# Expert attention: transposed second forming of the scores against row probabilities that TensorE transposes

## The reference, cut to what matters

```python
def _encoder_layer(x, iw, ib, ow, ob, l1w, l1b, l2w, l2b, n1w, n1b, n2w, n2b):
    b, s, d = x.shape                 # s = 112, d = 256
    hd = d // H                       # H = 16 heads of 16
    qkv = x @ iw.T + ib
    q, k, v = jnp.split(qkv, 3, axis=-1)
    rs = lambda t: t.reshape(b, s, H, hd).transpose(0, 2, 1, 3)
    q, k, v = (rs(q), rs(k), rs(v))
    scores = jnp.einsum('bhqd,bhkd->bhqk', q, k) / jnp.asarray(hd, x.dtype) ** 0.5
    attn = jax.nn.softmax(scores, axis=-1)
    o = jnp.einsum('bhqk,bhkd->bhqd', attn, v).transpose(0, 2, 1, 3).reshape(b, s, d)
    o = o @ ow.T + ob
    x = _layernorm(x + o, n1w, n1b)
    ff = jax.nn.relu(x @ l1w.T + l1b) @ l2w.T + l2b    # inner width 1024
    return _layernorm(x + ff, n2w, n2b)
```

## Time and profile before

| | |
|---|---|
| median of 3 runs | 3894.98 us |
| profiled execution | 3896.07 us |
| its span | 3894.4 us |
| TensorE busy | 3612.2 us, 93% |
| VectorE busy | 1980.3 us, 51% |
| ScalarE busy | 1434.1 us, 37% |
| POOL busy | 371.6 us, 10% |
| mean granted TensorE clock | 0.967 |
| expert stage, first to last TensorE work | 2734.7 to 3883.4 us |

### The profile page before, as it was taken

The page is one execution under the profiler, slowest core; times in us unless marked ns, Lnnn a source line. Parts: engine busy times, 40 slices in busy tenths (PEclk is TensorE's granted clock), DMA queues, the critical chain, the costliest instruction groups (busy, mean ns, idle before and its releaser), DMA issues. The chain is left out here.

```text
span 3894.4 us, 81102 instructions
## 1 busy us (share of the span) xinstructions
PE 3612.2 (93%) x32871; PEld 2736.2 (70%) x32871; DVE 1980.3 (51%) x5378; ACT 1434.1 (37%) x3167; POOL 371.6 (10%) x455
## 2 busy tenths in 40 slices
PE   6999999999699898989898989994899999999997
PEld 4777777777576666666666666662788887878886
DVE  3665656566235353535353534452455555556554
ACT  2343344334134233333333343432344443444443
POOL 1111111111000000000000000000011111111111
PEclk9999999999699999999999999997899999999999
DMA  2000000000200001010101010001300001110000
GB/s 76 12 12 13 14 12 12 14 14 8 88 11 13 24 11 25 9 27 9 28 5 31 1 35 1 25 1 54 129 16 12 11 17 50 54 52 12 15 12 8
DMA packets 63555, 94.55 MB, mean 24 GB/s; under 512 B 7762, under 2 KB 59602, under 8 KB 62146
## 3 DMA queue, kind: packets, MB, share of 16 engines
q1 hardware_dynamic: 55074, 83.41, 6.9%
q0 software_dynamic: 8224, 7.36, 1.7%
HBM read 72.07 MB, written 18.37 MB: 23 GB/s over the span
## 5 line engine op out<-in xcount | busy, mean ns | idle before, releaser
L1478 PE MATMUL bps<-BXT,Bwexp 128*128 128x112 f32 x3072 | 379.7, 282 | 6.2 <-DMA Bwexp<-in_we 3.6
L1478 PEld LDWEIGHTS bps<-BXT,Bwexp 128*128 128x128 f32 x3072 | 361.7, 195 | 22.1 <-issue 9.3
L1243 DVE CUSTOM_DVE_ANT_0 PON<-pps,PMR 112x375 f32<-112x375 f32 x512 | 259.7, 544 | 194.3 <-PE pps L967 192.9
L1096 ACT ACTIVATE PPT<-pps,mcol 125x896 f32<-125x896 f32 x192 | 192.4, 1007 | 204.6 <-PE pps L986 204.4
L1564 PE MATMUL bps<-Bwexp,BPT 128*112 128x256 f32 x1024 | 235.9, 380 | 0.0
L657 POOL TENSOR_TENSOR rstd<-var,nhalf 112x1 f32<-112x1 f32 (+1 forms) x96 | 148.3, 1545 | 838.6 <-DVE var L575 459.1
L967 PE MATMUL pps<-PKT,PQM 64*112 64x375 f32 x1024 | 211.1, 501 | 6.0 <-DVE Pmx L1243 4.0
L1276 POOL TENSOR_TENSOR Prstd<-Pvar,nhalf 112x1 f32<-112x1 f32 x128 | 70.1, 548 | 1517.9 <-DVE Pvar L1164 1517.9
L1618 ACT ACTIVATE BPT<-bps,Bwexp 128x112 f32<-128x112 f32 x512 | 139.1, 354 | 170.9 <-PE bps L1478 170.9
L1564 PEld LDWEIGHTS bps<-Bwexp,BPT 128*112 128x112 f32 x1024 | 174.5, 177 | 35.3
L986 PE MATMUL pps<-PQM,PKT 64*125 64x448 f32 x768 | 187.5, 567 | 0.0
(11 more groups left out here) (302 smaller groups left out, 7280.8 us busy)
## 6 DMA issues: line engine op xcount, KB each, us to landing
Bwexp<-in_we SPq DMA_DIRECT2D x7, 2304.0 KB, 17.0
PCX<-in_ctx SPq DMA_DIRECT2D x32, 375.0 KB
BXIN<-xmid SPq DMA_DIRECT2D x64, 112.0 KB
out<-BY POOLq DMA_DIRECT2D x64, 112.0 KB, 2.9
Bwexp<-in_we SPq DMA_DIRECT2D x7, 777.0 KB, 4.6
wa_sb<-in_wa SPq DMA_DIRECT2D x1, 4736.0 KB, 14.8
Brexp<-in_re SPq DMA_DIRECT2D x7, 672.0 KB
XIN<-in_x SPq DMA_DIRECT2D x32, 112.0 KB
```

Of the source, the lines that this page charges most:

```text
L1096: A(PT[s][0:KP, k, :, :].rearrange("p (i v) q -> p i (v q)", i=2), PS[s][0:KP, :, 0:QW], ACT.Exp, bias=mcol[:, k, bass.ds(at.n[s] + s * qu ...
L1243: m = v.tensor_tensor_reduce(out=ON[s][0:T, i * LC:(i + 1) * LC], in0=bank[s][i][0:T, 0:LC], in1=MR[s][:, :], scale=1.0, scalar=-3.0e38, o ...
L1478: m = mm(o[:, j * T:(j + 1) * T], wt[:, c, n0 + j * 128:n0 + (j + 1) * 128], rhs[:, c, :], start=(c == 0), stop=(c == 1))
```

## The change

Scores are formed once, with the queries in the partitions. Of each half of eight heads VectorE takes the maxima and multiplies them by -0.25 (low). ScalarE then runs one exp a head (112x112) with low as its bias column and accum_out for the row sums, so eight for a half. VectorE takes the reciprocal of the sums and multiplies the half by it in place. TensorE transposes eight heads at a time back into the lane's banks, ScalarE copies each half to PT. The values lie in V48, 48 columns for two heads: 16 of the one, 16 zeros, 16 of the other. A window of 32 of these columns is the weights of one head, and two heads add into the same 32 partitions. The product thus comes out with its features in the partitions, and OT is read from it directly. Gone are the transposed maxima, the selector matmuls, the second forming of the scores, the ones column, the transposes back to rows, ON and its transposes.

The diff, without the semaphore names and with the tables of three engines:

```diff
@@ -84,27 +84,27 @@
-    "lead3": (0, 264, 500, 764),
...
+    "lead3": (0, 262, 500, 762),
...
+    "pe3": ((30, 71, 245, 266, 466, 515, 687, 756, 775, 837, 875, 904, 987, 988,),
+            (30, 42, 106, 285, 371, 523, 610, 737, 757, 826, 883, 883, 960, 976,),
+            (30, 89, 255, 270, 436, 496, 555, 578, 800, 969, 979, 979, 996, 996,),
+            (30, 74, 171, 287, 479, 595, 644, 790, 819, 854, 889, 889, 898, 898,)),
+    "act3": ((0, 79, 204, 259, 491, 491, 705, 743, 791, 861, 888,),
+             (8, 25, 132, 320, 395, 510, 560, 602, 797, 913, 945,),
+             (1, 40, 225, 348, 391, 497, 568, 586, 817, 919, 955,),
+             (1, 32, 103, 338, 519, 593, 730, 761, 839, 846, 877,)),
+    "dve3": ((10, 85, 220, 250, 456, 702, 720, 720, 915, 974,),
+             (52, 210, 259, 259, 321, 593, 607, 665, 851, 923,),
+             (68, 278, 315, 375, 432, 612, 626, 834, 834, 870,),
+             (10, 150, 313, 351, 493, 730, 732, 779, 782, 860,)),
...
@@ -1338,17 +1338,15 @@
             XIN, X, Y = lanes("XIN", [T, D]), lanes("X", [T, D]), lanes("Y", [T, D])
             XT, KT = lanes("XT", [128, C2, T]), lanes("KT", [128, C2, T])
             QM = lanes("QM", [128, C2, 4, T])
-            V32 = lanes("V32", [T, H, 32])
+            V48 = lanes("V48", [T, H // 2, 48])
             PT = lanes("PT", [128, H, T])
-            MXB, MXT = lanes("MXB", [T, 128], BF16), lanes("MXT", [128, T], BF16)
-            mx, rec = lanes("mx", [T, H]), lanes("rec", [T, H])
+            mx, low, sums, rec = lanes("mx", [T, H]), lanes("low", [T, H]), lanes("sums", [T, H]), lanes("rec", [T, H])
             st6, mv, var, rstd = lanes("st6", [T, 6]), lanes("mv", [T, 2]), lanes("var", [T, 1]), lanes("rstd", [T, 1])
 
             ZT, OT = XT, KT
             upper = [PT[s][0:T, 8:16, :].rearrange("p h q -> p (h q)") for s in LANES]
             ON, Z, ZN = ([a[:, k * D:(k + 1) * D] for a in upper] for k in range(3))
             HT = [PT[s][:, 0:FT, :] for s in LANES]
-            OS = [QM[s][:, 0, :, :] for s in LANES]
             onehot = ON[0][0:B, 0:E * NI].rearrange("p (e n) -> p e n", e=E)
             listf, listi = sa("listf", [3, NI]), sa("listi", [2, NI], I32)
 
@@ -1500,47 +1498,32 @@
                             t.wait(masked_ready[s], 2)
                             t.wait(vx_read[s])
                         else:
-                            t.wait(mx_ready[s])
+                            t.wait(exp_ready[s])
                         for v in range(4):
                             for i in range(2):
                                 m = mm(bank[s][i][0:T, v * T:(v + 1) * T], QM[s][side[i], c, v, :], KT[s][side[i], c, :], start=True, stop=True)
                         m.then_inc(s_psum[s], 1)
 
-                    yield
-                    t.wait(mx_ready[s])
-                    mm(b0[:, 0:T], MXB[s][:, :], identb, start=True, stop=True).then_inc(mt_psum[s], 1)
-
-                    for c in range(C2):
-                        yield
+                    for c in range(C2):
+                        yield
+                        t.wait(soft_ready[s])
                         if c == 0:
-                            t.wait(mt_ready[s])
+                            t.wait(exp_ready[s])
                         else:
-                            t.wait(p_ready[s])
+                            t.wait(pt_ready[s])
                         for v in range(4):
                             for i in range(2):
-                                mm(bank[s][i][0:T, v * T:(v + 1) * T], msel[side[i], 4 * c + v, 0:T], MXT[s][side[i], :],
-                                   start=(v == 0), stop=False, skip_group_check=True)
-                        for i in range(2):
-                            m = mm(bank[s][i][0:T, 0:QW], KT[s][side[i], c, :], QM[s][side[i], c, :, :], start=False, stop=True, skip_group_check=True)
-                        m.then_inc(st_psum[s], 1)
-
-                    yield
-                    t.wait(p_ready[s])
-                    for g in range(4):
-                        for i in range(4):
-                            h = 4 * g + i
-                            m = mm(b0[32 * i:32 * i + 32, g * T:(g + 1) * T], V32[s][:, h, :], PT[s][0:T, h, :],
-                                   start=(g == 0), stop=True, skip_group_check=True)
-                    m.then_inc(sp_psum[s], 1)
-
-                    yield
-                    t.wait(sp_ready[s])
-                    for g in range(4):
-                        m = transpose(b1[0:T, g * 128:(g + 1) * 128], OS[s][:, g, :], ident)
-                    m.then_inc(so_psum[s], 1)
-                    yield
-                    t.wait(on_ready[s])
-                    transposes(ON)
+                                m = transpose(bank[s][i][0:T, v * T:(v + 1) * T], PT[s][0:T, 8 * c + 4 * i + v, :], ident[0:T, 0:T])
+                        m.then_inc(pt_psum[s], 1)
+
+                    yield
+                    t.wait(pt_ready[s])
+                    for c in range(C2):
+                        for n in range(2):
+                            for k in range(4):
+                                m = mm(b0[32 * k:32 * k + 32, c * T:(c + 1) * T], V48[s][:, 4 * c + k, 16 * n:16 * n + 32],
+                                       PT[s][0:T, 8 * c + 2 * k + n, :], start=(c == 0 and n == 0), stop=(n == 1), skip_group_check=True)
+                    m.then_inc(o_psum[s], 1)
                     yield
                     t.wait(late_in[s], 16)
                     t.wait(tp_ready[s])
@@ -1587,21 +1570,25 @@
                     m.then_inc(kx_read[s], 1)
                     yield
                     t.wait(qkv_psum[s])
-                    A(V32[s][:, :, 0:16], b0[0:T, 0:D].rearrange("p (h d) -> p h d", h=H), ACT.Copy).then_inc(vx_read[s], 1)
-
-                    yield
-                    t.wait(mt_psum[s])
-                    A(MXT[s][:, :], b0[:, 0:T], ACT.Copy).then_inc(mt_ready[s], 1)
-                    for c in range(C2):
-                        yield
-                        t.wait(st_psum[s])
+                    A(V48[s][:, :, :].rearrange("p k (n d) -> p k n d", n=3)[:, :, 0:3:2, :], b0[0:T, 0:D].rearrange("p (k n d) -> p k n d", k=8, n=2),
+                      ACT.Copy).then_inc(vx_read[s], 1)
+
+                    for c in range(C2):
+                        yield
+                        t.wait(top_ready[s])
+                        for i in range(2):
+                            for v in range(4):
+                                h = 8 * c + 4 * i + v
+                                m = A(PT[s][0:T, h, :], bank[s][i][0:T, v * T:(v + 1) * T], ACT.Exp, scale=0.25, bias=low[s][:, h:h + 1],
+                                      accum_out=sums[s][:, h:h + 1])
+                        m.then_inc(exp_ready[s], 1)
+                    for c in range(C2):
+                        yield
+                        t.wait(pt_psum[s])
                         A(PT[s][0:T, 8 * c:8 * c + 8, :].rearrange("p (i v) q -> p i (v q)", i=2), PS[s][0:T, :, 0:QW],
-                          ACT.Exp, scale=0.25).then_inc(p_ready[s], 1)
-                    yield
-                    t.wait(sp_psum[s])
-                    A(OS[s], b0[:, 0:QW].rearrange("p (g q) -> p g q", g=4), ACT.Copy).then_inc(sp_ready[s], 1)
-                    yield
-                    t.wait(tp_psum[s])
+                          ACT.Copy).then_inc(pt_ready[s], 1)
+                    yield
+                    t.wait(o_psum[s])
                     for m2 in range(C2):
                         m = A(OT[s][:, m2, :], b0[:, m2 * T:(m2 + 1) * T], ACT.Identity, bias=wc(s, "bv")[:, m2:m2 + 1])
                     m.then_inc(tp_ready[s], 1)
@@ -1631,9 +1618,7 @@
 
                 v.memset(items[:, NI:], -1)
                 for s in LANES:
-                    v.memset(V32[s][:, :, 16:17], 1.0)
-                    v.memset(V32[s][:, :, 17:32], 0.0)
-                    v.memset(MXB[s][:, :], 0.0)
+                    v.memset(V48[s][:, :, 16:32], 0.0)
                 v.memset(onesq[:, :], 1.0)
                 dve.wait_ge(route_dma, 16 * 2)
                 dve.wait_ge(added, 16)
@@ -1707,22 +1692,14 @@
                     for c in range(C2):
                         yield
                         t.wait(s_psum[s])
-                        top = v.tensor_reduce(mx[s][:, 8 * c:8 * c + 8], PS[s][0:T, :, 0:QW].rearrange("p i (v k) -> p i v k", v=4), AX_X, ALU.max)
-                        if c == 0:
-                            top.then_inc(mx_ready[s], 1)
-                    chained(top)
-
-                    m3 = mx[s][:, :].rearrange("p (c i v) -> p i c v", c=2, i=2)
-                    high, low = [MXB[s][:, :].rearrange("p (i n c v) -> p i n c v", i=2, c=2, v=4)[:, :, n, :, :] for n in range(2)]
-                    t.wait(mx_ready[s])
-                    chained(v.tensor_copy(high, m3))
-                    v.tensor_tensor(low, m3, high, ALU.subtract).then_inc(mx_ready[s], 1)
```

(22 more changed lines are left out.)

## The result

| | before | after |
|---|---|---|
| median, 14 runs each | 3891.96 us | 3900.53 us |
| profiled execution's span | 3894.4 us | 3902.3 us |
| steady round of the expert stage | 69.65 us | 68.9 us |
| TensorE busy / idle in a steady round | 69.5 / 0.1 us | 64.6 / 4.3 us |

The ratio after to before is 1.0023, with a 95% interval of 1.0013 to 1.0033: slower by 8.6 us, where 3843 us was forecast, 49 less than before. The steady round did become shorter, by 0.77 us and not by 3.45, and the rest of the stage lost more than that again.

The account below looks back on a forecast made before the run. TensorE's full stream was taken to bound the expert stage at 69.65 us a round; 63.7 plus 2.5 of stalls gives 66.2, so -55 over 16 rounds, +3 for filling and draining: 3843 us, range 3800 to 3930 (forecast's own 3815 to 3880).

Parts of the forecast that it names:

- What TensorE loses and gains: TensorE's expert-stage round: 12.3 us of groups removed, 6.3 us of new transposes added, net 6.0 off, leaving 63.7 us.
- the rival of half the clock: TensorE's new transposes run at half the clock, 6.3 us more a round, 3944 us; chance 0.05.
- E: ScalarE's time for eight 112x112 exps, each with its accumulator read; taken as 2.8 us, a period of 0.335.
- The rivals that put the slow side on this price: ScalarE's exps wait for reads to end: 3.6 us per eight, 3934, chance 0.20; no overlap: 4.3, 4027, chance 0.07.
- the break-even of 0.39 us: ScalarE's period per exp at which TensorE's stalls use up the 6.0 us it saves, E about 3.25.
- Where ScalarE makes TensorE wait: Walk of the new step order in the expert stage: TensorE stalls behind ScalarE's exps, 2.5 us a round at E 2.8.
- v of lane d: TensorE after s0a waits for KTd behind XTd, cp0b and exp0a on ScalarE: E - 1.6, called the worst place.
- values c: TensorE after s0b waits for copy cp1c behind OTd, XTa and exp0b on ScalarE: late by E - 1.8.
- Lane b's relus: TensorE's l2 of b, after s0d, waits for relus behind KTc and exp0d on ScalarE: late by E - 2.55.
- VectorE at nothing: VectorE's two added products an item (1.09 us each) are covered, 48 of 64 us a round busy, costing nothing.
- SP at nearly nothing: SP's loads, issued in another order, cost nearly nothing; two or three TensorE groups precede the lane's XIN transposes.
- Filling and draining: Filling and draining the expert stage's lanes changes by 0 to 5 us; 3 us added to the time.

Follow-up runs that it names:

- the new tables: Changed kernel, all instructions kept, with program-searched turn tables (order of steps) on all five engines of the expert stage: 3793.1 us, ratio 0.9746.
- one step moved: Changed kernel with lane c's first maxima put ahead of lane a's layer norm on VectorE: 3883.0 us, ratio 0.9967.
- neither sums nor product: Changed kernel without the exps' accum_out row sums and without VectorE's product by the reciprocal: 3848.4 us, ratio 0.9878.

## Why the prediction was wrong

- **What TensorE loses and gains: right to within 1 us.** 63.7 us a round was worked out. The changed kernel is busy for 64.6, 0.9 more; under the new tables, where it never waits, it takes 63.1. A block of eight transposes is 0.77 from start to start in that run, at a granted clock of 1.00:

```profile
...
3054.16 0.93 PE L1516 MATMUL bps<-const,BPT 112*112 112x112 f32 x8
3054.93 1.94 PE L1547 MATMUL bps<-Bwexp,BPT 128*112 128x256 f32 x8
...
```

The Trainium skill (TensorE: Matmul & The Clock Gate, Part 4: PE-mode transpose) says that a transpose doesn't count as PE busy in the same way and that the full clock doesn't engage for it. In the steady rounds here, with transposes among matmuls, the granted clock is 1.00, so the rival of half the clock is refuted.
- **E: right.** ScalarE's timeline of the changed kernel:

```profile
...
2992.74 0.37 ACT L1582 ACTIVATE BPT<-bps,Blow 112x112 f32<-112x112 f32 x1
2992.98 0.22 ACT L1582 ACTIVATION_READ_ACCUMULATOR BPT<-bps,Blow 112x1 f32 x1
2993.07 0.38 ACT L1582 ACTIVATE BPT<-bps,Blow 112x112 f32<-112x112 f32 x1
...
2995.28 0.27 ACT L1582 ACTIVATION_READ_ACCUMULATOR BPT<-bps,Blow 112x1 f32 x1
...
```

An exp starts every 0.33 us (0.335 taken), the read beginning 0.24 into it and the next exp 0.09 after that. Eight take 2.8. The rivals that put the slow side on this price were wrong, and so was the break-even of 0.39 us that I named as the deciding point: the kernel is slower at 0.33. (By the prediction's own terms the stalls at E = 3.25 sum to 5.3; they reach 6.0 only at an E of about 3.35, a period of 0.40.) The wide range of 3800 to 3930 holds 3900.5 by luck: its upper part stood for dearer exps, and they were not dearer.
- **Where ScalarE makes TensorE wait: this is the step that failed.** It gave 2.5 us a round for E = 2.8, and the idle time is 4.3. With the 0.9 of busy time over 63.7 that makes the 68.9 in place of 66.2. The two places that I priced high are there at their price, v of lane d (1.2 forecast, 1.0 measured) and values c (1.0 and 0.7). Three of the five were missed: the second scores of lane c (0.9), pt0 of lane c (0.8, where 0.1 was forecast) and q and k of lane c (0.9). Lane b's relus, priced at 0.25, are not waited for. I walked two engines, TensorE and ScalarE, and took VectorE and SP as always in time. The run with other tables shows that these waits belonged to the order: with the same instructions they are 0.
- **VectorE at nothing: wrong.** The product was compared with VectorE's share of the round and with the place after it, not with what is queued behind it. Leaving it out took 1.1 us off a round.
- **SP at nearly nothing: wrong.** I priced the layer norm but not the 1.8 us from its end to q and k, in most of which SP reads, branches and signals. Moving the reads ahead gave 0.4 a round.
- **The changes of experts were not priced at all**, and the 8 to 11 us that they cost more are the size of the loss. Filling and draining: 3 forecast, about 7 measured, in one execution of each kernel.
- **The granted clock outside the steady rounds was not priced either.** It is at 0.50 for 22 us more of the stage than before, which lies within the two items above.

In sum, of the 57 us between 3843 and 3900, (68.9 - 66.2) x 16 = 43 are the steady rounds, counted 16 as in the prediction (29 of them the waits, 14 TensorE's busy time), 8 to 11 the changes, and 4 the edges.

Why the loads at a change are waited for longer is only partly shown. With SP reading ahead, the excess of the rounds with a change falls from 19.1 to 10.3 us in the changed kernel, from 10.6 to 3.7 in the kernel before and from 14.0 to 1.9 with the new tables, so SP's reading looks like a part of it, with one execution of each and the clock moving too. With the new tables TensorE waits for no load directly, yet those rounds stay 14.0 us longer; no run moved the distance from a lane's go to its q and k alone.

## What to carry to other kernels

Where every engine runs a fixed order, the work saved on the full engine is about the most that a round can gain, and it is reached only when the other engines' steps stand at the right places: the same instructions took 3900.5 or 3793.1 us. A walk of such an order must take every engine that signals, with what is queued ahead of each step, and an experiment that leaves work out and gains much does not show that the amount of that work was the cause; repeat it under another order. Compare two designs only with tables found in the same way. Look at the granted clock of the stretches that are not steady: a stall there can be followed by work at half the clock.

## What the runs showed of the hardware

A ScalarE accumulator read behind an exp of 112x112 lasts 0.235 us in the mean but adds only 0.085 to the distance between exps (0.33 against 0.245 without it). Within the run of eight shown above, the exps' recorded durations grow from 0.37 to 0.42 and the reads' from 0.22 to 0.27 while the distance stays 0.33, so a sum of the durations would overstate E by nearly two.

After a stall of 5.18 us for weights, the next 6.34 us of TensorE's work ran at a granted clock of 0.50; the stalls of 0.7 to 1.0 us in the steady rounds left it at 1.00.

TensorE's busy time depends on the order of its groups. It is 64.6 us a round in the changed kernel and 63.1 under the new tables, with the same matmuls. The stalls themselves explain little of the 1.5 us: with one of the five gone (one step moved) it is still 64.6, and with three gone and a fourth down to 0.3 (neither sums nor product) it is 64.15. What the rest is, no run shows. Five rounds of each of these two:

```profile
2790.00:3129.82 339.82, 322.85 (x3120) 278.07 (x3120) 239.74 (x541) 232.73 (x1001) 40.61 (x62) 1.00 0.09 14
2795.38:3122.10 326.72, 320.75 (x3120) 277.88 (x3120) 197.62 (x502) 204.44 (x681) 40.28 (x61) 1.00 0.09 14
```
